# The first layer's preparation as one program block, and the end of its attention joined to the attention's own block

## The reference, cut to what matters

```
q, ma = quant4(x)                       # per token: ma = max|x|, q = clip(round(x/ma*7), -8, 7)
sign, alpha = ternary_weight(Wqkv)      # sign is 0 where |w| < 0.05*mean|w|; alpha is mean|w| of a row
p = (q @ sign.T) * ma/7 * alpha + bias  # one projection serves as query, key and value
queries = rotary(p); keys = rotary(p by chunks of the sequence); values = p by chunks
scores use U @ U.T between query and key; softmax over 512 keys; 16 heads of width 8
y = quant4(heads) @ ternary(Wo).T * ma/7 * alpha_o
x = layernorm(x + y)
```

## Time and profile before

| | |
|---|---|
| three runs | 1803.74, 1805.57, 1805.57 us; median 1805.57 |
| profiled execution | 1804.04 us, span 1802.1 us from the first to the last instruction |
| PE busy | 1502.6 us, 83% of the span |
| DVE busy | 1066.7 us, 59% |
| ACT busy | 640.5 us, 36% |
| POOL busy | 211.6 us, 12% |

### The profile page before, as it was taken

How to read it: one execution, slowest core, us unless ns; L and a number is a source line. 1 busy time by engine, 2 the same in 40 slices (tenths; PEclk the granted TensorE clock), 3 DMA queues, 4 the chain that set the end, 5 groups by cost and what they waited for, 6 DMA issues and landing times. The chain is left out here.

```text
span 1802.1 us, 22144 instructions
## 1 busy us (share of the span) xinstructions
PE 1502.6 (83%) x8176; PEld 690.0 (38%) x8176; DVE 1066.7 (59%) x2630; ACT 640.5 (36%) x920; POOL 211.6 (12%) x227
## 2 busy tenths in 40 slices
PE   1699689994668889999988998998988679996885
PEld 0333244442223434446443233354436423334353
DVE  4696455456964667763544882555445556745354
ACT  1266252213325023332423663422212145552431
POOL 2000010001000534332000000000000103331000
PEclk9899689996978889998997998997987679998798
DMA  5000000003000010000002000000010000000000
GB/s 205 0 1 1 1 1 1 1 0 137 0 1 1 0 47 1 2 1 1 1 11 93 1 1 1 1 1 1 1 70 1 1 0 1 1 2 1 1 1 12
DMA packets 4074, 27.14 MB, mean 15 GB/s; under 512 B 384, under 2 KB 2432, under 8 KB 2944
## 3 DMA queue, kind: packets, MB, share of 16 engines
q1 hardware_dynamic: 2912, 25.22, 3.5%
q10 hardware_dynamic: 1056, 0.52, 0.1%
HBM read 25.21 MB, written 0.52 MB: 14 GB/s over the span
## 5 line engine op out<-in xcount | busy, mean ns | idle before, releaser
L833 DVE TENSOR_REDUCE maxima<-banks 128x1 f32<-128x512 f32 (+4 forms) x640 | 363.1, 604 | 107.7 <-PE banks L682 100.8
L977 ACT ACTIVATE big<-banks 128x1024 f32<-128x1024 f32 (+2 forms) x320 | 294.4, 960 | 264.8 <-PE banks L725 93.9
L710 PE MATMUL banks<-big 32*128 32x512 f32 (+6 forms) x1280 | 232.2, 612 | 17.2 <-DVE big L854 12.9
L682 PE MATMUL banks<-big 32*128 32x77 bf16 (+6 forms) x1024 | 157.9, 296 | 23.6 <-ACT big L238 6.1
L1444 DVE TENSOR_TENSOR big<-big,banks 128x512 f32<-128x512 f32 (+1 forms) x116 | 79.8, 688 | 151.8 <-PE banks L1357 146.4
L746 PE MATMUL banks<-big,v_heads 128*9 128x512 f32 (+7 forms) x1024 | 159.6, 569 | 6.3 <-ACT heads_out L893 3.2
L466 POOL TENSOR_TENSOR rstd<-mean_var,minus_half 128x4 f32<-128x4 f32 x34 | 34.9, 1025 | 1036.2 <-DVE mean_var L396 1036.2
L1419 ACT ACTIVATE big<-banks 128x512 f32<-128x512 f32 (+1 forms) x116 | 69.1, 596 | 178.6 <-PE banks L1356 178.4
L682 PEld LDWEIGHTS banks<-big 32*128 32x128 bf16 (+1 forms) x1024 | 57.1, 97 | 180.5 <-DVE maxima L833 92.8
L1387 PE MATMUL banks<-big,moe_weights 128*128 128x512 f32 (+1 forms) x232 | 118.9, 597 | 3.0 <-ACT big L1427 2.6
L710 PEld LDWEIGHTS banks<-big 32*128 32x128 f32 (+3 forms) x1280 | 72.8, 178 | 70.1 <-ACT big L977 23.7
(11 more groups left out here) (406 smaller groups left out, 2211.7 us busy)
## 6 DMA issues: line engine op xcount, KB each, us to landing
moe_weights<-in_moe SPq DMA_DIRECT2D x1, 4864.0 KB, 15.3
moe_weights<-in_moe SPq DMA_DIRECT2D x1, 4768.0 KB, 21.6
moe_weights<-in_moe SPq DMA_DIRECT2D x1, 3264.0 KB, 10.2
moe_weights<-in_l3x SPq DMA_DIRECT2D x1, 3072.0 KB, 9.9
late_weights<-in_l2x SPq DMA_DIRECT2D x1, 2048.0 KB, 7.9
moe_weights<-in_l SPq DMA_DIRECT2D x1, 1234.0 KB, 12.8
rows<-in_rows SPq DMA_DIRECT2D x1, 1152.0 KB, 8.1
late_weights<-in_turned SPq DMA_DIRECT2D x1, 1152.0 KB, 17.9
```

Of the source, the lines that this page charges most:

```text
L682: last = nc.tensor.matmul(RING[n % NR][:, x * klen:x * klen + last_key(t)], q[rows, t * P:(t + 1) * P], ks[rows, 0:last_key(t)], start=Tru ...
L710: last = nc.tensor.matmul(SC[pair % 2][0:size, j % 2, n0:S], ks[rows, i * P:i * P + size], q[rows, n0:S], start=True, stop=turned)
L833: nc.vector.tensor_reduce(dst, src, AX_X, ALU.max).then_inc(ring_free.up(), 1)
L977: nc.scalar.activation(E[pair % NEP][0:size, :, n0:S], SC[pair % 2][0:size, :, n0:S], ACT.Exp, scale=scale).then_inc(exp_ready.up(), 1)
```

## The change: what it does, and the diff

- One block, `begin`, takes the place of the eleven. SP still issues the same loads in the same order. DVE and ACT wait for the pack `const`, DVE and PE for `first`, DVE for `x`, for the vectors and for `mid`, each where it is used.
- Both ternary weights go through one chain (256 columns wide instead of twice 128).
- `quantise` becomes `quantised_half`, four tiles each. The first half stands ahead of the thresholds, the second behind the signs. The other constants of `const` are copied while ACT and PE turn the second half.
- The query rotations move from DVE to POOL, which writes its products to other memory. All 16 value cuts go to ACT (ten before, six after the keys); ACT also takes seven of the 16 key cuts.
- PE turns the 32 key tiles first and the eight query tiles last.
- The end of the first attention is handed to `row_attention` as `finish`. `Front` has a new field `make`, called ahead of each `turn_front`, which quantises a half of the heads; PE waits for `front_made`.

The diff, cut to its core; the deleted functions stand in the listing above:

```diff
+        if self.front.make:
+            pe.wait_ge(self.front_made.sem, self.front_made.at(half + 1))
...
-    def dve_first(self, dve):
+    def dve_first(self, dve, heads_done=None):
...
+            if self.front.make:
+                if heads_done:
+                    heads_done(dve, 0)
+                self.front.make(dve, self.step, 0).then_inc(self.front_made.up(), 1)
...
-    def dve_rest(self, dve):
+    def dve_rest(self, dve, heads_done=None):
...
+        if self.front and self.front.make:
+            if heads_done:
+                heads_done(dve, 1)
+            self.front.make(dve, self.step, 1).then_inc(self.front_made.up(), 1)
...
+def quantised_half(c, dve, step, src, half):
+
+    vector, ts = c.nc.vector, slice(half * ST, (half + 1) * ST)
+    t1, r7, amax = c.total, c.rstd, c.amax
+    seq(dve, step, vector.tensor_reduce(amax[:, ts], src[:, ts, :], AX_X, ALU.max, apply_absolute_value=True))
+    seq(dve, step, vector.tensor_scalar(amax[:, ts], amax[:, ts], 1e-6, None, ALU.max))
+    seq(dve, step, vector.reciprocal(r7[:, ts], amax[:, ts]))
+    for t in range(half * ST, (half + 1) * ST):
+        last = vector.tensor_scalar(t1[:, t, :], src[:, t, :], r7[:, t:t + 1], 7.0, ALU.mult, ALU.mult)
+    vector.tensor_scalar(amax[:, ts], amax[:, ts], 1.0 / 7.0, None, ALU.mult)
+    seq(dve, step, last)
+    seq(dve, step, vector.tensor_scalar(t1[:, ts, :], t1[:, ts, :], ROUND, ROUND - 8.0, ALU.add, ALU.max))
+    return vector.tensor_scalar(c.q_bf[:, ts, :], t1[:, ts, :], ROUND, 7.0, ALU.subtract, ALU.min)
...
+def begin(c, x_loaded, vectors_loaded, load):
...
+    pieces = [(bl, cl) for bl in range(4) for cl in range(4)]
+
+    def rotate(eng, own_step, dst, ts, cos, sin, whole, memory):
+        p5 = proj.rearrange("p t (h i two) -> p t h i two", h=HEADS, two=2)
...
+        for k, (x, y) in enumerate(((t1, cos), (t2, sin), (t1, sin), (t2, cos))):
+            last = eng.tensor_tensor(view(room[k]), x, y, ALU.mult)
+        seq(eng, own_step, last)
+        eng.tensor_tensor(out[:, :, :, 0, :], room[0], room[1], ALU.subtract)
+        return eng.tensor_tensor(out[:, :, :, 1, :], room[2], room[3], ALU.add)
...
+        block.sync(load)
...
+            pool.wait_ge(projected.sem, projected.at(1))
+            for b in range(B):
+                rotate(nc.gpsimd, pool_step, c.XN, slice(b * ST, (b + 1) * ST), cos, sin, False, c.big1).then_inc(queries_rotated.up(), 1)
+                if b == 0:
+                    pool.wait_ge(queries_rotated.sem, queries_rotated.at(1))
...
+            pe.wait_ge(sign_moved.sem, sign_moved.at(1))
+            for half in range(2):
+                pe.wait_ge(q_moved.sem, q_moved.at(half + 1))
+                for k in range(ST):
+                    t = half * ST + k
+                    last = nc.tensor.matmul(c.bank[2 + 2 * half][:, k * P:(k + 1) * P], c.qT_bf[:, t * P:(t + 1) * P], c.signT[:, 0, :], start=True, stop=True)
+                last.then_inc(product_ready.up(), 1)
+            pe.wait_ge(keys_cut_act.sem, keys_cut_act.at(1))
+            pe.wait_ge(keys_cut_dve.sem, keys_cut_dve.at(1))
+            for u in range(KU):
+                for i in range(4):
+                    last = nc.tensor.transpose(c.bank[u][:, i * P:(i + 1) * P], key_tiles[:, 4 * u + i, :], c.ident[:])
+                last.then_inc(turned_ready.up(), 1)
+            for half in range(2):
+                pe.wait_ge(queries_rotated.sem, queries_rotated.at(half + 1))
+                s = dve_freed if half else act_freed
+                pe.wait_ge(s.sem, s.at(1))
+                for k in range(ST):
...
+            act.wait_ge(c.loaded["const"], 16)
+            nc.scalar.copy(c.ident[:], c.m("ident")).then_inc(ident_ready.up(), 1)
             for half in range(2):
+                act.wait_ge(q_turned.sem, q_turned.at(half + 1))
+                nc.scalar.copy(c.qT_bf[:, half * S:(half + 1) * S], c.banks_bf[5 + half][:, 0:S]).then_inc(q_moved.up(), 1)
+            act.wait_ge(projected.sem, projected.at(1))
+            for bl, cl in pieces[:10]:
+                cut_value(bl, cl)
+            act.wait_ge(keys_rotated.sem, keys_rotated.at(1))
+            act.wait_ge(room_ready.sem, room_ready.at(3))
+            for bl, cl in pieces[:7]:
+                last = cut_key(nc.scalar.copy, bl, cl)
+            last.then_inc(keys_cut_act.up(), 1)
+            for u in range(0, KU, 2):
+                act.wait_ge(turned_ready.sem, turned_ready.at(u + 1))
+                nc.scalar.copy(K[:, u * S:(u + 1) * S], c.bank[u][:, :]).then_inc(act_freed.up(), 1)
+            act.wait_ge(turned_ready.sem, turned_ready.at(KU + 1))
+            nc.scalar.copy(c.q32[:, 0, 0:S], c.bank[0][:, :])
+            for bl, cl in pieces[10:]:
+                cut_value(bl, cl)
...
+            dve.wait_ge(c.loaded["const"], 16)
+            vector.tensor_copy(c.ident_bf[:], c.m("ident"))
+            dve.wait_ge(c.loaded["first"], 16)
+            seq(dve, step, vector.tensor_reduce(rows, w, AX_X, ALU.add, apply_absolute_value=True))
+            seq(dve, step, vector.tensor_scalar(rows, rows, 1.0 / P, None, ALU.mult))
+            dve.wait_ge(ident_ready.sem, ident_ready.at(1))
+            for z in range(2):
+                last = vector.tensor_scalar(diag[:, z, :], c.ident[:], rows[:, z:z + 1], None, ALU.mult)
+            last.then_inc(rows_ready.up(), 1)
+            dve.wait_ge(x_loaded, 16)
+            quantised_half(c, dve, step, c.X, 0).then_inc(quantised.up(), 1)
+            dve.wait_ge(total_ready.sem, total_ready.at(1))
+            vector.tensor_copy(c.alpha.rearrange("p z m -> p (z m)"), c.bank[1][:, 0:2 * P])
...
+            vector.tensor_tensor(above, above, below, ALU.subtract).then_inc(sign_ready.up(), 1)
+            quantised_half(c, dve, step, c.X, 1).then_inc(quantised.up(), 1)
+            dve.wait_ge(sign_turned.sem, sign_turned.at(1))
+            vector.tensor_copy(c.signT.rearrange("p z m -> p (z m)"), signs[:, 0:2 * P]).then_inc(sign_moved.up(), 1)
+            vector.tensor_copy(c.key_later[:], c.m("later"))
...
+            dve.wait_ge(vectors_loaded, 32)
+            for half in range(2):
+                ts = slice(half * ST, (half + 1) * ST)
+                dve.wait_ge(product_ready.sem, product_ready.at(half + 1))
+                for k in range(ST):
+                    t = half * ST + k
...
+                if half:
+                    last.then_inc(projected.up(), 1)
+                    dve.wait_ge(projected.sem, projected.at(1))
+                else:
+                    seq(dve, step, last)
...
+            rotate(vector, step, c.total, slice(0, NT), *[tab_k[:, z].unsqueeze(1).broadcast_to([P, NT, HEADS * 4]) for z in range(2)], True, c.big2).then_inc(
+                keys_rotated.up(), 1)
+            dve.wait_ge(keys_rotated.sem, keys_rotated.at(1))
+            dve.wait_ge(room_ready.sem, room_ready.at(3))
+            for bl, cl in pieces[7:]:
+                last = cut_key(vector.tensor_copy, bl, cl)
+            last.then_inc(keys_cut_dve.up(), 1)
+            for u in range(1, KU, 2):
+                dve.wait_ge(turned_ready.sem, turned_ready.at(u + 1))
+                vector.tensor_copy(K[:, u * S:(u + 1) * S], c.bank[u][:, :]).then_inc(dve_freed.up(), 1)
+            dve.wait_ge(turned_ready.sem, turned_ready.at(KU + 2))
+            vector.tensor_copy(c.q32[:, 0, S:2 * S], c.bank[1][:, :])
...
+    attention_8(c, [P] * ST, 8.0 ** -0.5, chunked=True, projections=projections,
+                needs={(b, k): b * 4 + k + 1 for b in range(B) for k in range(4)},
+                finish=lambda: Norms(c, product_of(c, c.qT_bf[:].unsqueeze(1), c.signT[:, 1, :]), [Norm(c.X, turned=[(c.XT, None, None)])],
+                                     front=Front(c.q_bf, c.qT_bf, True, lambda dve, step, half: quantised_half(c, dve, step, c.Y8, half)),
+                                     weigh=weigh))
...
-                sp.wait_ge(x_loaded, 16)
-                sp.wait_ge(vectors_loaded, 32)
-                for pack in ("first", "mid", "early"):
-                    sp.wait_ge(c.loaded[pack], 16)
...
+            sp.wait_ge(c.loaded["mid"], 16)
+            sp.wait_ge(c.loaded["early"], 16)
+
+        begin(c, x_loaded, vectors_loaded, load)
```

More of the change, by code:

```diff
@@ L1263, in layer0_attention @@
-    keys = c.big3(4 * TOK, 4 * TOK).rearrange("p (t i bl d) -> p t i bl d", t=NT, bl=4, i=4)
-    with nc.Block() as block:
-        @block.vector
-        def _(dve):
-            for bl in range(4):
-                for cl in range(4):
-                    src = c.total[32 * bl:32 * bl + 32].rearrange("p t (i cl d) -> p t i cl d", i=4, cl=4)[:, :, :, cl, :]
-                    nc.vector.tensor_copy(keys[32 * cl:32 * cl + 32, :, :, bl, 0:8], src)
     Q, K = heads_8(c, S)
-    turn(c, c.XN[:], NT, P, c.q32)
@@ new lines, in load @@
+        def load(sp):
+            sp.dma_start(c.X[:], x_in).then_inc(x_loaded, 16)
+            for pack in ("const", "first"):
+                c.fetch(sp, pack)
```

(6 more changed lines are left out.)

265 lines of the change are left out of this document (86 added, 179 removed).

## The result

The changed kernel takes 1779.19 us in the median of four runs (1778.98 to 1781.90), the kernel before 1804.91 on the same chip (1803.74 to 1805.57). The ratio is 0.9862 with a 95% interval of 0.9845 to 0.9879, so it is faster by 25.7 us, 1.4%. The forecast was 1782 with a range of 1774 to 1789.

A forecast was written before the change was run, and what follows sets the result against it. The opening was taken as a chain of waits with no engine full. Gains of 19.8 (opening) and 4.6 (attention's end) less 1.5 (clock) made 22.9 us: 1781.1 from the profiled 1804.04, forecast median 1782, range 1774 to 1789.

The forecast's parts named there:

- two dates: Claim: the attention's first product start (63.84 us before) and the weighing's start relative to the attention's end decide the gain.
- Opening: Start to the attention's first product: one block removes waits, first product at 44.0 instead of 63.84, gain 19.8 us.
- the interlock: POOL's query rotation holds up DVE's key rotation and cuts: 0.45 us per POOL instruction, 5.4 for twelve, ends 2.3 and 8.8.
- both rivals on this term: POOL and DVE hardly disturb each other (1779 us, chance 0.2), or exclude each other fully (1785 us, chance 0.17).
- hardly disturb: Rival: POOL costs DVE only 0.19 us per instruction in the opening, 3.1 us less, 1779; chance 0.2.
- POOL late: Rival: POOL's stepped query rotation takes 2.0 us per instruction, ends at 45, opening gives 5 to 6 less, 1788; chance 0.1.
- Hides nothing: Rival: the opening's waits return inside the block; four of 4 us or more would bring it to 1804; chance 0.01.
- Tail: First attention's end: half-wise quantising lets the weighing start at 186.45 instead of 191.05, gain 4.6 us.
- Clock: PE's hole of about 3 us before the attention may move a clock fall: 1.5 us lost, ends 3.5 lost, 2.8 gained.
- the old place: The clock fall at 79.01 us in the kernel before, which the moved hole might spare, gaining 2.8 us.
- the 0.9 that I had named as a limit: Sign: the prediction is wrong if the first attention's clock lies below 0.9 on average.
- the rival with the attention at a low clock: Rival: the first attention stays at the low clock, slower than before, 1806 us and more; chance 0.02.

The follow-up runs named there:

- e1: Changed kernel with one added wait: POOL starts the query rotation only after DVE's nine key cuts; 1775.73 us, ratio 0.9841.
- e6: Changed kernel with the first half of x quantised behind the signs instead of ahead of the thresholds; 1784.25 us, ratio 0.9897.
- e2: Changed kernel plus 24 unread PE transpositions filling PE's idle time before the attention; 1777.32 us, ratio 0.9849.
- e3: Changed kernel with ACT's last six value cuts made by POOL behind its rotation; 1777.86 us, ratio 0.9849.
- e10: Changed kernel with queries rotated on DVE behind its key cuts, and the last six value cuts on POOL behind the key cuts; 1771.42 us, ratio 0.9818.
- f0: The changed kernel run once more, unedited, beside the delayed kernels; 1780.60 us, ratio 0.9870.
- e4: Changed kernel's opening, with the first attention's end in separate blocks as in the kernel before; 1790.04 us, ratio 0.9926.
- e5: Changed kernel with DVE awaiting x, the vectors and the packs first, mid and early before its first sum; 1789.27 us, ratio 0.9920.
- f6: Changed kernel with six needless one-column DVE instructions ahead of its first sum, a pure delay; 1781.85 us, ratio 0.9886.
- f12: Changed kernel with twelve needless one-column DVE instructions ahead of its first sum, a pure delay; 1782.04 us, ratio 0.9882.

## Why the prediction was right, step by step

**Bounds.** That two dates decide holds: at the start of the weighing the changed kernel is ahead by 22.79 us of its 24.6 (the traced spans; the medians differ by 25.7).

**Opening, 21.44 instead of 19.8: the mechanism was right, single terms were off.** The projection was ready at 20.77, 0.48 sooner than forecast. The cut keys were ready at 32.31, forecast 33.8. Of the 1.49 between them 0.48 is the projection, 0.63 the interlock (4.77 measured, 5.4 forecast, 0.40 for each POOL instruction and not 0.45), and 0.35 was added in my sum without a reason: 28.05 + 5.4 is 33.45. The 40 transpositions took 6.99 us (32.46 to 39.45), forecast 7.2. From the last of them to the attention it was 2.95, forecast 3.0. The value cuts, 2.47 forecast, took 2.46.

**The interlock** was the term with the widest ends (2.3 and 8.8), and e1 measured it at 4.77. The side-by-side row of one-input copies was therefore too low, and adding all of POOL's time too high. Both engines slow down: a pair of multiplications takes 1.1 us, where one behind the other would take 0.684 + 0.624 = 1.31. So both rivals on this term fall by their size, though "hardly disturb" (1779) named the median that came: that time was met by luck, by an opening 1.64 us and a rest 1.81 us better than forecast. The Trainium skill, "SBUF — State Buffer", section "Summary: rules for kernel authors", has the second of the two to issue blocked fully until the first finishes, when VectorE's has two SBUF inputs and GpSimd's reads SBUF. These rows show more than half of that (0.42 us onto DVE's 0.684 beside a partner of 0.624), and not all.

**POOL late** fell: twelve instructions ended at 31.26 (forecast 33 to 35), PE wanted the first of them at 38.41. **Hides nothing** fell: DVE has no wait from 7.20 to the projection's end. I said that PE's totals lie beside the first half's quantisation, and e6 shows what they cost without it, 1.81 (forecast 1.31). That rival's own price was also too low: four waits of 4 us are 16, and to undo 22.9 they would have to be 5.7 each.

**Tail, 4.73, forecast 4.6.** The term was right by its own steps, and the last heads were not late.

**Clock: -3.4 instead of -1.5, inside the ends (3.5 lost, 2.8 gained); this is the step that failed most.** I set the loss between a fall at the hole and a fall spared at the old place. Both falls happened: the first group took 18.83 and the second is at 0.58. e2, e3 and e10, in which the hole is 0.34 to 1.64, have first groups of 15.72 to 15.87 us; with holes of 2.00 and more they lie between 17.46 and 20.31. That is four executions (the kernel before, with 1.05 and 15.72, is the fourth) against ten, with none out of line; of these e2 alone changes nothing else, so it carries the claim that the hole is the cause. How long the clock stays low isn't set by the hole's length: at the same 2.95 us the low stretch is 6.83 us long in the changed kernel and 10.23 in f0, its twin (43.10 to 53.33, at 0.50), and the first groups are 17.46, 18.84 or 20.2 us long. What sets it is open. Over the first attention the clock was 0.93 (18.83 us at 0.82 and 104.14 at 0.95), above the 0.9 that I had named as a limit, and the rival with the attention at a low clock fell.

**The rest, +1.8, was not in the sum.** It can't be counted as an effect of the change: f0's rest is 1611.54, longer than before.

In sum, 21.44 + 4.73 - 3.38 + 1.81 = 24.6, against 22.9 forecast. The errors of the opening (+1.64), the clock (-1.88) and the rest (+1.81) partly cancel.

**Open:** why the rest takes 1607.9 to 1617.3 us for the same instructions. The low clock in the trace goes with it: behind the weighing it lasts 337 us in e10, with the shortest rest, 340 in the changed kernel and 361 to 363 in e2, e4 and e5, with the longest. f6 and f12 show that a delay needn't change it; the four times of e2 and of e6 suggest that it changes from one execution to the next of one program.

## What to carry to other kernels

When an opening is a chain of blocks with a full engine nowhere, add up the busiest engine's own work from the first load that it truly needs; that sum held here within 2 us over 35. In these runs work handed to GpSimd was free only where VectorE wasn't the path: put it under a stretch of TensorE's work, not beside the chain that TensorE waits for. Judge a gain of a few microseconds in the dates of the trace next to the median, because the stages far behind can differ by more than that, even between executions of one program.

## What the runs showed of the hardware

- VectorE and GpSimd multiplying side by side, both with two inputs: VectorE's went from 684 to 1104 ns, GpSimd's from 624 to as much as 1070 ns. VectorE's one-input copies of 32x256 beside GpSimd rose from 0.298 to 0.546 us each (2.68 and 4.91 for nine).
- A GpSimd multiplication of 256 columns in rows of four stepping by two took 624 ns, less than the 734 of an unstepped one with a mask.
- After 2.95 us of idle time ahead of a busy stretch TensorE's granted clock fell to 0.53 for 6.83 us; over the first group it was 0.96 after 0.34 us, and 1.00 from 34.00 to 52.00 around it after 1.64 us.
- The same instructions, from the weighing on, took 1607.9 to 1617.3 us in the fourteen profiled executions here, of thirteen programs that differ only ahead of it; in one stage of them 18.70 us at 0.68 became 24.00 at 0.51.
